# A fused attention and mixture-of-experts block: four groups of instructions moved in the middle stage

## The reference

```
h   = layernorm(x) * (1 + ca) + sa
q   = kernel(h + h Wq),  ks = kernel(h + h Wk[k]),  vs = h + h Wv[k]     k = 0, 1; kernel = silu + 0.5
q, ks normalised per head of 16 channels
state = prod_k (ks_k^T vs_k)                  per head, 16 x 16, over all tokens
out = q state;  out = layernorm(out) @ Wo     (linear attention)
x   = x + ga * out
h   = layernorm(x) * (1 + cb) + sb
scores = sigmoid(h @ gate_w + bias);  the two best of 8 experts, weights normalised
shared = (gelu(h @ sw_up) @ sw_down) * 0.1    256 -> 1024 -> 256, all tokens
routed = sum over the two experts of w * 0.1 * (gelu(h @ up_w[e]) @ down_w[e])
y   = shared + routed;  y = y / (max|y| + 1e-6);  x = x + gb * y
```

## Time and profile before

| | |
|---|---|
| median of 3 runs | 949.35 us (944.55 to 950.42) |
| profiled execution, time | 939.66 us |
| its span | 937.8 us |
| TensorE, mean granted clock | 0.976 |
| busy: TensorE, VectorE, ScalarE, GpSimd | 853.0, 633.9, 474.1, 403.0 us |
| matmuls | 5989 |
| HBM over the span | 93 GB/s |

### The profile page before, as it was taken

How to read it: one execution, slowest core, us unless ns; L and a number is a source line. 1 busy time by engine, 2 the same in 40 slices (tenths; PEclk the granted TensorE clock), 3 DMA queues, 4 the chain that set the end, 5 groups by cost and what they waited for, 6 DMA issues and landing times. The chain is left out here.

```text
span 937.8 us, 21404 instructions
## 1 busy us (share of the span) xinstructions
PE 853.0 (91%) x5989; PEld 780.7 (83%) x5990; DVE 633.9 (68%) x1675; ACT 474.1 (51%) x880; POOL 403.0 (43%) x415
## 2 busy tenths in 40 slices
PE   6999999899989788799979999989999999999980
PEld 5778878788878677688779999989999999999980
DVE  5789986659777668578767666567665566666652
ACT  3866554253643534435456555455554455555530
POOL 3543500304243151342602655654566565555564
PEclk9999999899999999999999999999999999999995
DMA  8120000822232141230572322353333343344542
GB/s 283 67 91 1 1 1 1 261 60 72 57 104 51 67 116 23 93 88 28 207 255 59 101 75 77 85 174 74 73 87 88 87 92 90 71 86 77 100 84 48
DMA packets 68609, 83.31 MB, mean 89 GB/s; under 512 B 23088, under 2 KB 56842, under 8 KB 68400
## 3 DMA queue, kind: packets, MB, share of 16 engines
q0 software_dynamic: 25792, 39.92, 18.5%
q1 hardware_dynamic: 41920, 41.64, 14.3%
q10 hardware_dynamic: 816, 0.79, 0.3%
HBM read 45.44 MB, written 41.55 MB: 93 GB/s over the span
## 5 line engine op out<-in xcount | busy, mean ns | idle before, releaser
L1847 PE MATMUL psUp<-eT,wup 128*128 128x256 f32 x1632 | 206.0, 286 | 8.1 <-issue 4.6
L1847 PEld LDWEIGHTS psUp<-eT,wup 128*128 128x128 f32 x1632 | 199.8, 193 | 12.7 <-issue 11.5
L1873 PE MATMUL psY<-wdn,gTh 128*128 128x256 f32 x1088 | 199.3, 285 | 0.0
L1873 PEld LDWEIGHTS psY<-wdn,gTh 128*128 128x128 f32 x1088 | 168.4, 191 | 0.0
L1873 PE MATMUL psY<-wdn,gTl 128*128 128x256 f32 x544 | 153.6, 282 | 0.0
L1930 ACT ACTIVATE ys<-yc,meta 128x256 f32<-128x256 f32 x68 | 30.9, 502 | 181.9 <-DVE yc L1997 139.6
L2120 POOL DMA_INDIRECT out<-fin,oidx x68 | 109.1, 1604 | 21.6 <-issue 17.1
L1911 ACT ACTIVATE gu<-psUp,ubias 128x256 f32<-128x256 f32 x272 | 113.3, 468 | 4.5 <-PE psUp L1847 3.7
L1976 DVE TENSOR_TENSOR gTl<-gu,gTh 128x512 fp32r<-128x512 f32 x136 | 93.6, 688 | 29.9 <-ACT gTh L1916 20.6
L2110 POOL DMA_INDIRECT shared_part<-ys,widx x68 | 71.6, 1052 | 94.3 <-ACT ys L1930 54.7
L1161 PE MATMUL psU<-h2T,su 128*128 128x512 f32 x384 | 103.4, 408 | 9.4 <-ACT gf L1252 9.4
(11 more groups left out here) (297 smaller groups left out, 1435.6 us busy)
## 6 DMA issues: line engine op xcount, KB each, us to landing
hin<-expert_in SPq DMA_DIRECT2D x36, 256.0 KB
X<-in_L_attn_x SPq DMA_DIRECT2D x8, 512.0 KB, 7.7
X<-bo_row POOLq DMA_DIRECT2D x8, 512.0 KB
shared_part<-prow SPq DMA_DIRECT2D x8, 512.0 KB, 6.2
shared_part<-sh SPq DMA_DIRECT2D x8, 512.0 KB
out<-X SPq DMA_DIRECT2D x8, 512.0 KB
raw_up<-in_L_ffn_up_w SPq DMA_DIRECT2D x3, 1024.0 KB
raw_dn<-in_L_ffn_down_w SPq DMA_DIRECT2D x3, 1024.0 KB, 9.8
```

The costliest lines, as they stand in the source:

```text
L1847: mm = nc.tensor.matmul(psU[:, c, (m % 2) * TR:(m % 2 + 1) * TR], wup[s][:, a, k, m * P:(m + 1) * P], eT[:, u, b, k], start=(n == 0), stop ...
L1873: mm = nc.tensor.matmul(psE[:, u, h * C:(h + 1) * C], (gTh, gTl)[a][:, u, m, h * P:(h + 1) * P], wdn[s][:, b, m], start=(n == 0), stop=(n ...
```

## The change

Four instructions or groups of them change their place in a body, and nothing is added or taken away. On TensorE `chunk(1)`, which is the second up product, goes ahead of the second attention output. On ScalarE the sigmoid goes ahead of Gelu 1, with the table loads that belong to it. On VectorE low part 0 goes ahead of the reading of the second half, and the search goes ahead of low part 1. In body 0 there is no FFN and in body 8 no attention, and the orders there stay as they were.

```diff
--- before.py
+++ after.py
@@ -1189,9 +1189,9 @@
                 chunk(0)
                 if ffn_on:
                     turn_gate()
+                chunk(1)
                 if att_on:
                     outs(1)
-                chunk(1)
                 if not att_on:
                     rank()
                 if first:
@@ -1280,8 +1280,8 @@
                     return
                 if ffn_on:
                     gelu(0)
+                    score()
                     gelu(1)
-                    score()
                     gelu(2)
                     gelu(3)
                 if first:
@@ -1514,12 +1514,12 @@
                     gate_read()
                     if later(f, 1):
                         shared_read(f - 1)
+                low_g(0)
                 out_read(1)
-                low_g(0)
                 out_stats(1)
-                low_g(1)
                 if ffn_on:
                     best()
+                low_g(1)
                 if isinstance(g, int) and g == 1:
                     norm_read(3, NG)
                 out_norm()
```

## The result

The changed kernel is slower: 960.54 us median (957.86 to 962.0, four runs) against 946.95 (941.96 to 950.42) of the kernel before in the same set of runs, ratio 1.0162, 95% interval 1.013 to 1.0193. Its profiled execution has a span of 957.6 us against 937.8. Of the 19.8 us between them 16.8 lie between the first logits and the first expert's rows, in the stage that the change touches. The two traces lie further apart than the medians (13.6 us), because the traced execution of the kernel before, 939.66 us, was faster than all its untraced ones.

What follows compares the result with a forecast made beforehand. TensorE's late signals to ScalarE and VectorE were taken to bound bodies 2 to 7. A longer chain, 4.4 us, plus clock falls, 5.5, gave 9.9 us: 959.3 us median, 1.05% slower; range 936 to 964, the forecast's own 954 to 964.

Steps and rivals of the forecast that it cites:

- the sum: Whole kernel: 4.4 us for the longer chain plus 5.5 us for falls of the clock, 9.9 us slower.
- The late signal is bound to the time, not to the product: Body 5: the signal second in the new order, half 1's, arrives when the old second did, 347.7 rather than 343.5.
- rival A: Faster: half 1's reading gets its signal early, z transposes 3.4 us sooner in body 5; 937.6 us; chance 0.27.
- The chain behind it: Late signal, reading, statistics, search, low 1, down 1, up 4, z transposes: 8.20 us in loop bodies; loss 4.4 us.
- The sigmoid: ScalarE ahead of Gelu 1: load, sigmoid and load take 2.9 us, hidden in an idle stretch of 5.92 us.
- The clock: TensorE's idle stretch lowers the granted clock in bodies 4, 5, 6 and half in body 2: 3.5 x 1.57 = 5.5 us.
- Rival B: Slower as forecast, but the clock recovers while TensorE still waits: 953.8 us; chance 0.17.
- their terms: Bodies 3 to 6: chain loss 0.85 or 0.51 us each, plus 1.57 us per clock fall in bodies 4 to 6.
- Rival C: No effect: TensorE's signals are late only in part of the executions, both orders reach z transposes together; 949 us; chance 0.13.

Runs made afterwards that it cites:

- set 1: Runs with the kernel before at 928.91 us: TensorE's order undone 1.000, that order alone 1.002, low 1 ahead of the search again 0.9959, extra matmuls 1.0123.
- set 3: Runs against the kernel before, span 908.3 us: changed kernel 1.0066, TensorE's order undone 1.0019, the latter with residual rows stored early 1.0009.
- set 2: Runs with the kernel before at 911.97 us: changed kernel 1.0056, that with low 1 ahead of the reading 1.0129, kernel before with early residual stores 1.0007.

## Why the prediction was right

959.3 us was forecast and 960.54 measured, within the forecast's own range; the mechanism is the one forecast. That the totals agree to 1.2 us is partly luck: the loss was 13.6 us where the sum said 9.9, and the forecast counted from 949.35, while the kernel before had its median at 946.95 in the measured set.

*The late signal is bound to the time, not to the product.* This was the step chosen between two far ends (343.5 or 347.7). In body 5 the reading starts 11.4 us after the body's start (355.47 - 344.04); 11.3 was forecast. Bodies 4 and 6 both have 11.6. Gelu 2, which in bodies 2 to 6 starts with the reading, points the same way: the delay isn't that of one product. The trace of before could have said so. In its body 3 the reading and Gelu 1 started at 271.31 and 271.27, and the first signal was 3.0 us late in body 3 and 3.3 us in body 6; the 1.5 us that spoke for rival A were body 5's alone. So body 3, which the sum took as body 5, has the same distance to the z transposes but other signals. Signals don't always come at once: in body 5 before, the first came when up 1 had ended too, and that of up 1 4.2 us later. Rival A, which wanted the reading 4 us sooner, is refuted for that chip.

*The chain behind it.* From the reading to down 1 I had 5.23 us and the trace has 5.49. Most of the difference is that the statistics start 0.83 us after the reading and not 0.61, as low 0 no longer stands between them. That this chain is a loss even with signals on time is shown by the changed kernel in sets 2 and 3 (0.56 and 0.66%), and that the late reading makes it larger by the same pair of kernels with signals late (1.62%). That neither part loses so much alone is only suggested by set 1, where the signals of the kernel before aren't known; in set 3, with signals on time, TensorE's order undone leaves 0.19%.

*The sigmoid* and its loads took 2.8 us (349.43 to 352.26) where 2.9 was worked out, and TensorE didn't wait for Gelu 1 because of them. In the kernel with low 1 ahead of the reading they are not hidden: there VectorE waits for Gelu 1 behind them.

*The clock.* Falls came with the long idle stretches of bodies 2, 4, 5, 6 and 7, five where 3.5 were forecast, in bodies 4 to 6 of 6.8 us; in body 5 the fall cost 1.83 us (4.66 - 2.83) where 1.57 was taken. From down 1 to the z transposes the five take 8.3 us more than five times 2.83, where the sum had 5.5. Body 3 idled 2.97 us and had no fall. Rival B is refuted for that chip.

*What was mis-sized.* By bodies the loss is 0.1, 3.0, 1.2, 2.6, 2.9, 2.6 and 4.4 us (1 to 7), 16.7 in the traces against 9.9. With 8.3 us for the falls, 8.4 are left for the waits (an estimate, by difference) where the sum had 4.4, so both terms were too small. Bodies 3 to 6 lie 0.3 to 0.5 above their terms (0.85, 2.1, 2.4, 2.1). Most of the excess, 4.8 of 6.8 us, is in bodies 2 and 7: the reading came at 11.0 and 10.0 us after the body's start, where the second signal of before had come at 10.3 and 7.7, and both had a whole fall of the clock where half a one and none was priced. The tie of the signal to the time held to 0.2 us in the loop bodies and not there.

*Rival C* was given 0.13: lateness absent in part of the executions. It did not decide the measured result, but in sets 2 and 3 the lateness was absent, and the loss there is 0.6%. Its price, nothing, was wrong by about 1 us per loop body. It had both orders reach the z transposes at 351.6 in body 5, 15.2 us after the start; the new one does without lateness (15.3 in set 2), the old one comes at 14.1.

*What stays open.* What delays TensorE's signals. The transfers of body 5 are the same in number, bytes and place in the traces with and without the lateness, so they are not enough to cause it. The late trace itself says so too: at 190.0 to 192.2 us 190 GB/s moved, and the reading at 192.21 started 0.04 us after its product's recorded end. Whether they are needed was not shown, as the two kernels with earlier stores ran only where nothing was late. As the ends of matmuls are modelled, the traces also don't part a late signal from a product that in truth ended late. Whether any kernel beats the one before in every set is open too: 0.996 for low 1 ahead of the search was measured in set 1 alone.

## What to carry to other kernels

Before an instruction is moved ahead of a producer, list who stands behind it on its engine and when its own input comes in the worst execution, not in the usual one: the new orders, with a search of 2.8 us ahead of a low part of 0.7 us, cost about 1 us per loop body where the reading was on time and 2.6 to 2.9 us in bodies 4 to 6 where it was late, the low clock included. Moving a product behind another moves it into the other's delay, if the delay belongs to the time. And a long new idle stretch on TensorE is to be priced twice, once as the wait and once for the low clock that can come with it: five of the six stretches of 3.0 to 6.4 us had both here, and the waits of 1.0 to 1.6 us in sets 2 and 3 only the first.

## What the runs showed of the hardware

The end of a matmul in the trace and the arrival of its signal can lie far apart: 1.5 and 4.4 us in body 5 before; in two other sets of runs, with the same transfers there, the second of these signals came 0.04 us after the recorded end (the first can't be read, as VectorE was still busy). Two products' signals came through under 0.1 us apart in five of the six bodies with late ones: the reading at 355.47 and Gelu 2 at 355.42 in body 5 after. The kernel before took 947 to 949, 929 and 912 us in different sets, a spread of 4% that is larger than the change; of the 30 us between two of its traces, 19 lie in the stage with the late signals. In the changed kernel a granted clock of 0.50 lasted 6.8 us with idle stretches of 6.0 to 6.4 us and 3.4 us with those of 3.2 and 3.3 us; the length alone doesn't tell, as an idle 2.26 us preceded a fall in body 3 before and idle 2.23 and 2.97 us in body 3 after brought none. A table load does not wait for the input of its activation: in body 8 of the kernel before the load runs at 443.43, and its sigmoid starts at 449.02, after 4.31 us of waiting for the logits. Load, sigmoid and load took 2.8 us from the cast's end to the Gelu (349.43 to 352.26).
